# A four-layer graph network on one core: two passes over the edge records made into one, a later place for the gathers of run ends, and plain copies in the last section

## The reference

```
h = relu(layernorm(x))
x = x + L0(h)   # every edge: relu(pool_w (h[src] * (1 + coef*w)) + pool_b); maximum per node; concat with h; final_w
x = x + L1(h)   # four graph convolutions: hw = h @ W; sum over edges of dinv[src]*dinv[dst]*hw[src]; norm over all nodes
x = x + L2(h)   # sum per source node of relu(w1*v[dst]), relu(w2*edge_w), relu(W3 h[dst]); @ W4
x = x + L3(h)   # per source node: sum, maximum and mean of edge_attr[e]; two-layer perceptron
```

## Time and profile before

| | us |
|---|---|
| median of 3 runs (9850.27 to 9859.49) | 9859.22 |
| the profiled execution | 9877.71 |
| its span | 9875.9 |
| third pass, first to last transpose | 4618.8 to 5136.3 |
| attribute pass, first to last scan | 5178.3 to 5980.6 |
| POOL's cells, first to last scatter | 4583.0 to 6872.9 |
| POOL's gathers of run ends for it | 5201.6 to 5323.0 |

### The profile page before, as it was taken

The page is one execution under the profiler, slowest core; times in us unless marked ns, Lnnn a source line. Parts: engine busy times, 40 slices in busy tenths (PEclk is TensorE's granted clock), DMA queues, the critical chain, the costliest instruction groups (busy, mean ns, idle before and its releaser), DMA issues.

```text
span 9875.9 us, 151767 instructions
## 1 busy us (share of the span) xinstructions
PE 7070.4 (72%) x44134; PEld 5776.1 (58%) x44134; DVE 7036.8 (71%) x18590; ACT 4875.1 (49%) x7967; POOL 5380.0 (54%) x5426
## 2 busy tenths in 40 slices
PE   4444444424788887881656567996899899997998
PEld 3333333323666766661445455664799798896787
DVE  7888888733666666662558777775787777777777
ACT  1111111112555555551442336885788787785777
POOL 6777777777777777777777777776000000001120
PEclk5555555555777677675776888998999999999999
DMA  6666544444333333339995896775788888987999
GB/s 193 194 194 194 175 143 143 143 134 66 93 93 94 93 92 92 93 89 102 258 226 122 191 213 175 204 204 123 231 279 277 247 280 252 274 279 174 210 213 196
DMA packets 2775520, 1739.57 MB, mean 176 GB/s; under 512 B 1805046, under 2 KB 2613980, under 8 KB 2774660
## 3 DMA queue, kind: packets, MB, share of 16 engines
q1 hardware_dynamic: 2435460, 1298.36, 52.6%
q10 hardware_dynamic: 165920, 277.72, 8.1%
q0 software_dynamic: 173408, 154.46, 7.0%
HBM read 1065.70 MB, written 506.69 MB: 159 GB/s over the span
## 4 chain that ended last, share of the span: by engine, by line
POOL 43%; PE 18%; issue 18%; DMA 10%; DVE 6%; ACT 3%; SPq 1%; POOLq 0%; ACTq 0%; DVEq 0%
POOL adj L933 16%; POOL records L907 13%; PE PS L1341 12%; POOL G L853 11%; DMA raw_f<-adj 3%; PE PS L1531 3%; DMA pair_raw<-adj 2%; DVE OH L2135 2%; ACT ring_f L1847 1%; DMA G<-node_table,IDX 1%; DMA IDX<-in_src_q 1%; POOL fill_rows L869 1%; POOL AG L884 1%; POOL T L884 1%; DMA records<-RT,IDX 1%
## 5 line engine op out<-in xcount | busy, mean ns | idle before, releaser
L853 POOL DMA_INDIRECT G<-node_table,IDX x1664 | 1629.8, 979 | 557.9 <-issue 544.2
L933 POOL DMA_INDIRECT adj<-OH,EA x1664 | 1652.1, 993 | 507.3 <-issue 507.3
L907 POOL DMA_INDIRECT records<-RT,IDX x1664 | 1616.0, 971 | 518.5 <-issue 498.6
L1341 PE MATMUL PS<-ring_f,terms_r 128*128 128x448 f32 x8232 | 1706.5, 368 | 19.7 <-DVE ring_f L2665 9.8
L2665 DVE CAST ring_f<-raw_f 128x1792 fp32r<-128x1792 uint8 x1323 | 1408.2, 1091 | 386.5 <-DMA raw_f<-adj 251.1
L1847 ACT CAST ring_f<-raw_f 128x1792 fp32r<-128x1792 uint8 x882 | 1467.2, 1691 | 386.9 <-DMA raw_f<-adj 265.5
L1341 PEld LDWEIGHTS PS<-ring_f,terms_r 128*128 128x128 f32 x8232 | 1535.3, 188 | 180.3 <-ACT ring_f L1847 24.0
L1186 PE MATMUL PS<-R 98*128 98x128 f32 x3328 | 999.6, 394 | 0.0
L2142 DVE TENSOR_TENSOR_SCAN S<-M,S,PS 128x512 f32<-128x512 bf16 x621 | 791.0, 1274 | 258.6 <-ACT PS L1736 228.7
L1101 PE MATMUL PS<-OH 128*98 128x128 bf16 x3328 | 453.4, 317 | 626.3 <-DVE OH L2135 626.3
L950 POOL DMA_INDIRECT HC<-node_table,srow x21 | 30.6, 1458 | 1524.8 <-issue 1524.8
(11 more groups left out here) (415 smaller groups left out, 14501.7 us busy)
## 6 DMA issues: line engine op xcount, KB each, us to landing
raw_f<-adj SPq DMA_DIRECT2D x2205, 224.0 KB, 3.7
adj<-Z ACTq DMA_DIRECT2D x105, 1568.0 KB
AG<-adj SPq DMA_DIRECT2D x735, 224.0 KB
G<-records SPq DMA_DIRECT2D x624, 128.0 KB
M<-same_dst SPq DMA_DIRECT2D x416, 128.0 KB
fill_rows<-Z ACTq DMA_DIRECT2D x104, 512.0 KB, 2.9
runs_l<-R SPq DMA_DIRECT2D x208, 256.0 KB
G<-fill_rows SPq DMA_DIRECT2D x208, 256.0 KB
```

The source lines that it names most:

```text
L853: pool.indirect_dma_start(G[:, i, q * D:(q + 1) * D], None, table, bass.IndirectOffsetOnAxis(ap=IDX[:, i, q:q + 1], axis=0)).then_inc(sem( ...
L907: pool.indirect_dma_start(rec, bass.IndirectOffsetOnAxis(ap=IDX[:, i, q:q + 1], axis=0), RT[:, i, q, :], None).then_inc(sem(f"scattered{i} ...
L933: pool.indirect_dma_start(adj_cells, bass.IndirectOffsetOnAxis(ap=CELL[:, at:at + 1], axis=0), VAL[:, at:at + 1], None).then_inc(sem(f"cel ...
L1341: m = pe.matmul(half_of(x, h)[:, c, :], stat, RINGF[q % NR][:, h * QW + c * HW:h * QW + (c + 1) * HW], start=K == 0, stop=False, skip_grou ...
```

## The change

There are three edits.

- **One pass in place of two.** The third pass and the attribute pass are one loop over the 208 chunks on SP, PE, ACT and DVE. A mask is loaded once for both. The two chunk buffers of the attribute pass lie elsewhere (parts of `Z` and `L` instead of `G` and `R`), and four PSUM banks that each of the two loops used in pairs are now used singly: one for `fwd3`, one for `back3`, one each for the sums and maxima turned back. `cells_made(1)` comes behind the one loop.
- **The gathers of run ends.** POOL issues 23 groups of `adj_out` ahead of the wait for `srow_ready`, not 15. Then come the 98 gathers.
- **Copies.** For the last part of the table (tiles 672 to 734 of 735), DVE's share of the conversions is a plain `tensor_copy` and no longer a `scalar_tensor_tensor` that adds a zero from PSUM.

The core of the diff:

```diff
 # SP
+            def step3(c):
+                i = c % 4
+                if c >= 4:
                     sp.wait_ge(sem("fwd3"), c - 3)
                 for h in range(2):
                     rows = rec[bass.ds(c * CE + h * H, CE), :].rearrange("(k p) d -> p k d", p=P)
                     sp.dma_start(G[:, i, :]...[:, :, h, :], rows[:, :, 0:D]).then_inc(sem(f"block_in{i}"), 16)
                 if i % 2 == 0:
+                    if c >= 4:
+                        sp.wait_ge(sem("e_scanned"), 2 * (c - 2))
                     masks_in(same_src, c, i // 2, c + N3 - 2)
+                attr_in(c, c % 2)
+                if c >= 2:
+                    attr_out(c - 2, c % 2)
 # PE
+            for c in range(NCH):
+                fwd3(c)
+                attr_fwd(c, c % 2)
+                if c:
+                    back3(c - 1)
+                    attr_back(c - 1, (c - 1) % 2)
 # ACT
+            for c in range(NCH):
+                relu3(c)
+                attr_pen(c, c % 2)
+                if c:
+                    out3(c - 1)
+                    attr_copy(c - 1, (c - 1) % 2)
 # DVE
+            for c in range(NCH):
+                step3(c)
+                attr_scans(c, c % 2)
+            dve.wait_ge(sem("e_back"), NCH)
             cells_made(1)
...
 # POOL
-            adj_out(0, NB // 4 + 2)
+            adj_out(0, PT[1] // CB - 1)
             pool.wait_ge(*dve_at("srow_ready"))
             runs_done(2)
             ends(AG, runs64, endrow[1], NG, 0, NG)
...
-            adj_out(NB // 4 + 2, NB - 4)
+            adj_out(PT[1] // CB - 1, NB - 4)
 # DVE, first convolution
+                    if r * NR + i >= LAST_FROM:
+                        dve.tensor_copy(RING[i], RAW[i]).then_inc(sem("conv_d"), 1)
+                    else:
                         dve.scalar_tensor_tensor(RING[i], RAW[i], 1.0, NOTHING...)
```

More of the change, by code:

```diff
@@ L719, in _ @@
             carry_in(CR2[:, :], dbc(runs[H - 1:H, 0:D], P), 0)
[L721 to L724, removed]
+            for d in (NCH - 2, NCH - 1):
+                attr_out(d, d % 2)
             for x in range(2):
@@ L1252, in _, with fwd3 @@
             runs_carried(0)
[L1254 to L1258, removed]
+            def fwd3(c):
+                i = c % 4
+                pe.wait_ge(sem(f"block_in{i}"), c // 4 * 32 + (16 * NIT + 32))
+                if c:
+                    pe.wait_ge(sem("l3r"), c)
                 for k in range(KC):
-                    t = pe.transpose(bank(1 + 5 * (i % 2))[:, k * P:(k + 1) * P], G[:, i, k * P:(k + 1) * P], ident[:, :])
+                    t = pe.transpose(bank(1)[:, k * P:(k + 1) * P], G[:, i, k * P:(k + 1) * P], ident[:, :])
@@ L1727, in _, with relu3, out3 @@
             messages(NCH - 1, 3, 6)
-            def step3(it, i, first):
-                c = it * 4 + i
-                s = i % 2
+            def relu3(c):
                 act.wait_ge(sem("fwd3"), c + 1)
                 act.wait_ge(sem("scanned"), c + N3 - 1)
[L1736 to L1742, removed]
-                act.wait_ge(sem("back"), c + N3 - NCH + 1)
[L1744 to L1748, removed]
+                act.activation(bank(5 * (c % 2)), bank(1), ACT.Relu, bias=poolb[:, 0:1]).then_inc(sem("l3r"), 1)
+            def out3(c):
+                i = c % 4
+                act.wait_ge(sem("back"), c + N3 - NCH + 1)
+                act.wait_ge(sem(f"runs_out{i}"), (c // 4 + NIT) * 16)
+                act.copy(R[:, i, :], bank(3)).then_inc(sem("r_ready"), 1)
                 act.wait_ge(sem("r_ready"), c + N3 - NCH + 1)
@@ L2438, in _, with step3, attr_scans @@
             masks_made(1)
-            def step3(it, i, first):
-                c = it * 4 + i
-                s = i % 2
+            def step3(c):
+                i = c % 4
                 dve.wait_ge(sem("l3r"), c + 1)
-                masks_there(it, i, 2 * NIT)
+                masks_there(c // 4, i, 2 * NIT)
                 dve.wait_ge(sem("back"), c + N3 - NCH - 1)
                 dve.wait_ge(sem("scanned"), c + N3)
[L2448 to L2453, removed]
+                scan(i, c + N3, bank(5 * (c % 2)), ALU.mult, ALU.max, c == 0).then_inc(sem("scanned"), 1)
+            def attr_scans(d, x):
+                if d == 0:
+                    keep = 0.0, 0.0
+                else:
+                    keep = E_SUM[1 - x][:, CE - 1:CE], E_MAX[1 - x][:, CE - 1:CE]
+                dve.wait_ge(sem("e_fwd"), d + 1)
+                if positive(d - 1):
+                    dve.wait_ge(sem("e_back"), d - 1)
+                if positive(d):
+                    dve.wait_ge(sem("e_scanned"), d * 2)
+                dve.tensor_tensor_scan(E_SUM[x], e_mask(d), bank(2 + 4 * x), keep[0], ALU.mult, ALU.add).then_inc(sem("e_scanned"), 1)
+                dve.wait_ge(sem("e_pen"), d + 1)
+                dve.tensor_tensor_scan(E_MAX[x], E_PEN[x], bank(2 + 4 * x), keep[1], ALU.add, ALU.max).then_inc(sem("e_scanned"), 1)
+            for c in range(NCH):
+                step3(c)
+                attr_scans(c, c % 2)
+            dve.wait_ge(sem("e_back"), NCH)
             cells_made(1)
@@ L2460, in _ @@
             dve.sem_inc(sem("dve_at"), 1)
[L2462 to L2474, removed]
-                dve.tensor_tensor_scan(E_SUM[x], e_mask(d), bank(x), keep[0], ALU.mult, ALU.add).then_inc(sem("e_scanned"), 1)
-                dve.wait_ge(sem("e_pen"), d + 1)
-                dve.tensor_tensor_scan(E_MAX[x], E_PEN[x], bank(x), keep[1], ALU.add, ALU.max).then_inc(sem("e_scanned"), 1)
-            for d in range(*RUNS_E[0]):
-                attr_scans(d, d % 2, d == 0)
+            for x in range(2):
+                dve.wait_ge(sem(f"e_out{x}"), 8 * NCH)
             def make_b(g, s):
@@ L2510, in _ @@
             dve.sem_inc(sem("h_ready"), 1)
-            for d in range(*RUNS_E[1]):
-                attr_scans(d, d % 2, False)
-            for x in range(2):
-                dve.wait_ge(sem(f"e_out{x}"), 8 * NCH)
             for g in range(NG2):
```

103 lines of the change are left out of this document (25 added, 78 removed).

## The result

| | us | ratio to before |
|---|---|---|
| before, same runs | 9854.74 (9849.69 to 9859.49) | |
| changed kernel, median of 4 | 10174.55 (10158.25 to 10214.61) | 1.0328 [1.0312, 1.0345] |
| its profiled execution, and its span | 10179.68, 10177.9 | |

The changed kernel is 3.3% slower. The forecast of 10,103 us had the sign, the place and the mechanism; the measured time is 72 us above it, inside the range of 9,870 to 10,240 us.

The account below looks back on a forecast made before the run. POOL's unbroken issue of scatters was taken as the bound; a 254 us stall less 10 us for copies gave 10,122 us against the profiled 9877.7 us, so a median of 10,103 us, range 9,870 to 10,240 us.

Parts of the forecast that it names:

- The bound and the place of the wait: POOL issues scatters without a pause; after 23 groups, at 5520.7 us, it waits for the second cells.
- The threshold and the price of a chunk: T is one joined chunk's time; POOL does not stall up to 4.12 us, above it 208 x (T - 4.12).
- The ring: In the joined pass SP's write waits for ACT's copies, ahead of chunk k+3's loads; two chunks a turn, 5.34 us each.
- half of a mask's 1.09, as it is loaded every other chunk, 0.55: SP's mask load in a turn of two chunks, counted at half of 1.09 us, 0.55 us.
- The signs named for DVE: In the joined pass DVE is busy some 70%; its idle time ends on loads or PE's transposes, not its own scans.
- The check by transfers: DMA work of a joined chunk, 5.10 us, takes 4.72 to 5.54 us at the two earlier passes' shares.
- The copies: Plain copies for DVE's conversions in the last part save 10 us, with nothing and 23 us as ends.
- The earlier release, worth nothing: The first convolution starts at most some tens of us later and still waits for POOL; the stall is not made up.
- The sum against the profiled execution: Whole profiled execution: 9877.7 + 254 of stall - 10 for the copies = 10,122 us.
- No stall: Rival: in the joined pass loads run far enough ahead, DVE's 3.81 us is T; 9849 down to 9836 us; 12%.
- the short ring: Rival: joined pass loads land faster, PE's clock stays high; T 4.25 to 4.6 us, 9,876 to 9,949 us; 10%.
- Loads slowed by each other: Rival: DMA share can't exceed 0.92 and waits add to transfers; T over 6.0 us, above 10,240 us; 8%.

Follow-up runs that it names:

- mask behind, write on ACT: Changed kernel with the write of sums and maxima issued by ACT and the mask's loads behind the attribute columns' loads: 9876.65 us, ratio 1.0000, no stall.
- write on ACT: Changed kernel with the write of sums and maxima issued by ACT behind its copies, off SP's list: 9886.53 us, ratio 1.0014.
- write one later: Changed kernel with SP's write of chunk c-3 in place of c-2 behind the loads of chunk c: 9947.49 us, ratio 1.0072.
- mask behind: Changed kernel with SP issuing an even chunk's mask loads behind its attribute columns' loads, not ahead: 10063.19 us, ratio 1.0193.

## Why the prediction was right, and where its size was off

**The bound and the place of the wait: right.** POOL came to its wait at 5515.5 us, against 5520.7 us predicted, and it set the end: in all runs but that with the gathers alone the stretch from its last scatter to the end stayed within 2979 and 3003 us, while the last scatter's start ranged over 372 us. The slices of the page, which the prediction read first, do not show that bound: the other engines are busy in every slice too, in some more than POOL. What shows it is DVE's idle time at the end and these runs.

**The threshold and the price of a chunk: right.** 208 x (T - 4.12) can be set beside what was measured (T from 4650 to 5450 us, in the last two rows, whose passes last longer, from 4650 to 5800 us):

| run | T, us | 208 x (T - 4.12) | POOL's stall, us | ratio |
|---|---|---|---|---|
| mask behind, write on ACT | 4.14 | 4 | 0 | 1.0000 |
| write on ACT | 4.26 | 29 | 27 | 1.0014 |
| write one later | 4.55 | 89 | 90 | 1.0072 |
| mask behind | 5.01 | 185 | 182 | 1.0193 |
| the changed kernel | 5.74 | 337 | 333 | 1.0328 |
| copies undone | 5.91 | 372 | 365 | 1.0352 |

**The ring: the mechanism right, one term mis-sized.** The step that was off is "half of a mask's 1.09, as it is loaded every other chunk, 0.55". A mask is loaded for every second chunk, but a turn of the ring also covers two chunks, and it can always go through the same one. It does: PE waited for the even chunk's columns 100 times and hardly for the odd one's. Against the middle of the sum, the turn of 11.48 us has 0.61 us more for the mask with its gap, 0.21 us more for PE's transposes (3.44 us from the first to the end of the last), 0.17 us less for the landing (4.53 us), and 0.15 us more for the other pieces: together the 0.80 us between 10.68 and 11.48. The mean of the 64 turns, 11.69 us, splits nearly the same way: mask with its gap 1.18, landing 4.65, transposes 3.46 us. So T was 5.74 us and not 5.34 us, and the stall 333 us and not 254 us. Moving the mask out of the turn brought 1.35% by the ratios, 133 us, where 116 us were expected, and 173 us against the run with the copies undone on its own chip, not all of it the mask's own, as that section shows. The signs named for DVE came out less well: it was busy 64% and not some 70%, and its longest idle time ended on ACT's relu (258.4 us), behind PE's transposes, and not on those themselves.

**The check by transfers: wrong.** It gave 4.72 to 5.54 us and seemed to confirm the sum (the mask's 0.49 us in it is elapsed time, 0.53 us in the unit of the other terms, which changes little), but T lies above it, since the share fell to 0.88, below both of the shares taken from the earlier trace rows. A share that a pass reached while it waited is no price of a byte: the same transfers went through in 4.14 us, at a share of 1.18, as soon as SP's list let them.

**The copies** were put at 10 us. Their runs bound them at 11 us and do not tell them from nothing. The stretch behind POOL shrank by 19 us in the changed kernel; up to 11 us may be theirs, but the run with the copies undone kept 13 of the 19, and what made these stays open.

**The earlier release, worth nothing: right**, and shown by the run without a stall. In the changed kernel the convolution began at 6098.6 us, 43 us later than before, where "some tens" were forecast. That the moved gathers "cost the same 98 issues" was right for POOL. What they cost the convolution alone, 203 us, was not in the prediction; it did not matter only because the other edit takes the work away that stood behind them.

**The sum against the profiled execution:** 10,122 us predicted, 10,179.7 us measured. The difference of 58 us is 79 us more stall, less 9 us by which the end was shorter than taken, and less 12 us by which POOL's scatters began and ran earlier. That these two went the other way is luck. The range held, but not with much to spare: the five runs with the copies undone, which have the same pass, took up to 10,238 us, against its end at 10,240 us.

**The rivals.** No stall and the short ring did not come, though both came as soon as the ring was opened: 4.14 us a chunk is 0.02 us from the threshold that the one named, and 4.26 us lies in the other's 4.25 to 4.6 us. Loads slowed by each other is out, since the share rose.

## What to carry to other kernels

Where an engine issues loads and stores in order, a store that waits for the end of the pipeline makes its depth the distance in the list between that store and the next load, whatever the buffers would allow: look for the wait, then move the store to the engine that makes its data. When a ring's turn covers two items, write out the turn item by item; a cost that is paid every other item is then paid in every turn or in none. And two passes that already lay under another engine's work saved nothing here by being joined: the joined pass was free only up to the time at which that cover ended.

## What the runs showed of the hardware that was not expected

With two loads of 256-byte rows, a write and a mask a chunk, the DMA share and rate went from 0.86 and 201 GB/s (the run with the copies undone) to 1.18 and 290 GB/s (the run without a stall) with the order of the issues and the engine of one write alone. POOL's scatters did not notice: the 627 to 628 of them in the 800 us came at the same 1.27 us whether the share was 0.86 or 1.18. And the mean granted clock of PE went with the pass: 0.77 at 5.97 us a chunk, 0.84 at 5.01 us and 0.91 at 4.14 us. PE's part of a turn of the ring was 3.47 us in the first of these and 2.21 us in the second, so the part grew with the turn.
